# Attention: the maximum's pieces of two heads on separate halves of the array, diagonal blocks of four heads in one bank, pieces dealt out by columns

## The reference

```python
qkv = x @ w_qkv                                   # (4, 2048, 3, 16, 16)
Q, K = apply_rope(Q), apply_rope(K)
attn = jnp.einsum('bqhd,bkhd->bhqk', Q, K) * scale
attn = jnp.where(causal, attn, NEG_INF)
attn = jax.nn.softmax(attn, axis=-1)              # over 2048 keys, causal
out = jnp.einsum('bhqk,bkhd->bqhd', attn, V).reshape(B, S, dim)
return out @ w_proj + b_proj
```

## Time and profile before

| what | us |
|---|---|
| median of three runs | 3551.72 |
| the profiled execution | 3548.13 |
| its span in the profile | 3546.4 |
| TensorE busy | 3175.5 (90%) |
| VectorE busy | 2645.6 (75%) |
| ScalarE busy | 1569.4 (44%) |
| GpSimd busy | 763.4 (22%) |
| attention, from its first instruction to the last output's division | about 324 to 2151 |
| of it: the first group's maxima | 339 to 426 |

### The profile page before, as it was taken

The page is one execution under the profiler, slowest core; times in us unless marked ns, Lnnn a source line. Parts: engine busy times, 40 slices in busy tenths (PEclk is TensorE's granted clock), DMA queues, the critical chain, the costliest instruction groups (busy, mean ns, idle before and its releaser), DMA issues. The chain is left out here.

```text
span 3546.4 us, 64058 instructions
## 1 busy us (share of the span) xinstructions
PE 3175.5 (90%) x18948; PEld 1799.1 (51%) x18948; DVE 2645.6 (75%) x6114; ACT 1569.4 (44%) x2096; POOL 763.4 (22%) x619
## 2 busy tenths in 40 slices
PE   5885999999999999999999996764599999799998
PEld 3552233333333333333333334554588888678787
DVE  4885888888887888878788833887477777566666
ACT  1442166666666666666566672111244444211111
POOL 1775000000000000000000002777332323333332
PEclk8997599999999999999999997665799999899999
DMA  1776111111111111111111104553554545322222
GB/s 66 190 206 192 42 31 46 45 54 47 38 39 45 54 47 42 36 45 54 47 44 35 34 7 110 171 165 121 171 163 151 162 152 163 115 89 89 89 89 71
DMA packets 372705, 315.08 MB, mean 89 GB/s; under 512 B 99436, under 2 KB 359000, under 8 KB 372440
## 3 DMA queue, kind: packets, MB, share of 16 engines
q1 hardware_dynamic: 360152, 278.26, 26.6%
q0 software_dynamic: 12288, 33.57, 2.8%
HBM read 194.27 MB, written 116.92 MB: 88 GB/s over the span
## 5 line engine op out<-in xcount | busy, mean ns | idle before, releaser
L820 ACT ACTIVATE probs<-ps_s 128x1024 f32<-128x1024 f32 (+3 forms) x1280 | 1083.5, 894 | 728.6 <-PE ps_s L957 475.1
L947 PE MATMUL ps_m<-k_st,q_st 96*128 96x512 bf16 (+3 forms) x2560 | 838.0, 363 | 47.9 <-POOL k_st L801 30.9
L957 PE MATMUL ps_s<-q_st,k_st 98*128 98x512 bf16 (+3 forms) x2560 | 714.4, 352 | 27.0 <-issue 20.3
L973 PE MATMUL ps_o<-probs,vs 128*32 128x512 f32 (+3 forms) x5120 | 605.0, 545 | 0.0
L845 DVE CUSTOM_DVE_ANT_0 masked<-ps_m,mask_qk 128x512 bf16<-128x512 f32 (+3 forms) x1024 | 462.5, 489 | 163.1 <-PE ps_m L947 150.9
L947 PEld LDWEIGHTS ps_m<-k_st,q_st 96*128 96x128 bf16 x2560 | 215.3, 97 | 715.7 <-DVE piece_late L848 205.7
L848 DVE TENSOR_REDUCE piece_late<-ps_m 128x1 f32<-128x512 f32 x768 | 473.1, 681 | 30.5 <-PE ps_m L947 29.8
L848 DVE TENSOR_REDUCE piece_rest<-ps_m 128x1 f32<-128x512 f32 x768 | 475.0, 682 | 27.5 <-PE ps_m L947 18.7
L1218 POOL MEMSET zeros<- 128x1024 f32 x1 | 1.0, 956 | 1815.1 <-POOLq L670 1815.1
L957 PEld LDWEIGHTS ps_s<-q_st,k_st 98*128 98x128 bf16 x2560 | 242.2, 98 | 247.5 <-ACT probs L820 67.7
L962 PE MATMUL ps_s<-mask_kq,ident_b 128*128 128x128 bf16 x1024 | 204.4, 219 | 0.0
(11 more groups left out here) (226 smaller groups left out, 5423.2 us busy)
## 6 DMA issues: line engine op xcount, KB each, us to landing
qk_parts<-parts SPq DMA_DIRECT2D x128, 192.0 KB, 2.9
k_st<-qk_parts SPq DMA_DIRECT2D x384, 64.0 KB, 2.3
q_st<-qk_parts SPq DMA_DIRECT2D x384, 64.0 KB, 2.3
x_r<-expert_rows SPq DMA_DIRECT2D x39, 512.0 KB, 4.5
expert_made<-made SPq DMA_DIRECT2D x39, 512.0 KB, 3.0
x_in<-in_L_attn_x_dram SPq DMA_DIRECT2D x32, 512.0 KB, 4.6
v_ones<-v_out SPq DMA_DIRECT2D x64, 256.0 KB, 4.7
vs<-v_ones SPq DMA_DIRECT2D x64, 256.0 KB, 3.6
```

The source lines that it names most:

```text
L820: act.activation(probs[:, u % PSLOTS, 2 * pair:2 * pair + 2, j * P:ST], ps_s[:, pair, :, j * P:ST], ACT.Exp, scale=SCALE).then_inc(exp_don ...
L947: pe.matmul(ps_m[:, bank, 0:w], q_st[0:ROWS, slot, h, qi * P:(qi + 1) * P], k_st[0:ROWS, slot, h, kt * ST:kt * ST + w], start=True, stop=T ...
L957: last = pe.matmul(ps_s[:, pair, hh, j * P:ST], k_st[0:ROWS + MROWS, slot, h, kc * P:(kc + 1) * P], q_st[0:ROWS + MROWS, slot, h, qt * ST ...
L973: last = pe.matmul(ps_o[h * VW:(h + 1) * VW, j * P:ST], vs[:, slot, kc, h * VW:(h + 1) * VW], probs[:, u % PSLOTS, h, j * P:ST], start=(kc ...
```

## The change

It does four things.

1. The rows of the stacks are laid out anew. The three products that weigh most stand together. For an even head they are rows 0 to 47; for an odd head rows 64 to 111, its other three products are rows 16 to 63, rows 0 to 15 are zero, and the maximum's two rows are 112 and 113 (96 and 97 for an even head). Each load of 16 rows takes two heads instead of four, so a region has 24 loads instead of 12. Rows from 96 on are set to one and rows 0 to 15 of odd heads to zero at the start: for slot 0 by VectorE, for slot 1 by GpSimd. SyncE's first load waits for VectorE's three.
2. A piece of 512 or 384 columns is now one matmul over 48 rows, with the three main products alone: the maximum need not be exact. Two heads, an even and an odd one, form a unit of two pieces, in two banks, one on array rows 0 to 63 and one on 64 to 127. TensorE starts a unit when the bank of its second piece is free.
3. Pieces no longer hold the diagonal block. What is left of 256 columns stands with two heads in one bank, of 128 columns with four, with all products. The 16 diagonal blocks of 128 stand with four heads in one bank and their own column in `piece_late` or `piece_rest`; the mask is a bf16 matmul of 512 columns by the identity. So VectorE has 140 plain reduces instead of 160 pieces, and the masked form is gone.
4. The order on TensorE: both scores' pairs of a position now stand together, and units stand in two slots of a position, ahead of the scores and ahead of the values. They are dealt out by columns (`work`, `width`) instead of by count.

```diff
@@ -43,9 +44,12 @@
-ROWS = 96
-QPART = (0, 0, 0, 1, 1, 2)
-KPART = (0, 1, 2, 0, 1, 0)
+QPART = (0, 0, 1, 0, 1, 2)
+KPART = (0, 1, 0, 2, 1, 0)
+MAIN = 3
+HEAD_ROWS = ((0, 16, 32, 48, 64, 80), (64, 80, 96, 16, 32, 48))
+SHIFT_ROW = (96, 112)
+MAX_BASE = (0, 64)
...
-    PIECES = [(kt, qi, h) for kt in reversed(range(NQ)) for qi in reversed(range(TPS * kt, NT)) for h in range(HG)]
-    LATE_END = max(i for i, (kt, qi, h) in enumerate(PIECES) if qi >= LATE)
-    LATE_LAG = 8
+    Piece = namedtuple("Piece", "qi col k0 w h n")
+    TRI = {True: NQ, False: NQ - 1}
+    WIDE = {1: HG, 2: HG // 2, 3: 1, TPS: 1}
+
+    def units_of(kt, qi):
+
+        w = min(TPS, qi - TPS * kt) * P
+        if w == 0:
+            out = []
+        else:
+            n = WIDE[w // P]
+            parts = [Piece(qi, kt, kt * ST, w, h, n) for h in range(0, HG, n)]
+            out = [parts[0:2], parts[2:4]] if n == 1 else [[part] for part in parts]
+        if qi < TPS * (kt + 1):
+            out.append([Piece(qi, TRI[qi >= LATE], qi * P, P, 0, HG)])
+        return out
+
+    UNITS = [unit for kt in reversed(range(NQ)) for qi in reversed(range(TPS * kt, NT)) for unit in units_of(kt, qi)]
+    FIRST_OF = {units_of(kt, NT - 1)[0][0]: kt for kt in range(NQ)}
+    LATE_END = max(i for i, unit in enumerate(UNITS) if unit[0].qi >= LATE)
+    LAST_LATE = UNITS[LATE_END][-1]
+    LATE_LAG = 3
...
-    LOADS = 2 * len(QPART)
+    LOADS = 4 * len(QPART)
...
+    def work(unit):
+        return sum((what.w * what.n if isinstance(what, Piece) else P) + P for what in unit)
 
     def plan_of(first, maxima):
 
 
-        spread = with_late(PIECES) if maxima else []
-        out = []
+        spread = with_late() if maxima else []
+        out = [[] for _ in range(2 * NPOS)]
+        width = [ST - P * max(0, kc - TPS * qt) + P for qt, kc in POSITIONS]
+        at = [0]
         for u in range(NPOS):
-            a, b = (len(spread) * (u - 1) // (NPOS - 1), len(spread) * u // (NPOS - 1)) if u else (0, 0)
-            now = spread[a:b]
-            if u == 1:
-                now = ["turn rest"] + now
-            if u == 3 and not first:
-                now = now + [("turn o", -1, NQ - 1)]
-            if u - 2 in LAST_OF:
-                now = now + [("turn o", 0, LAST_OF.index(u - 2))]
-            out.append(now)
+            at += [at[-1] + width[(u + 1) % NPOS], at[-1] + width[(u + 1) % NPOS] + width[u]]
+        total, past = sum(work(unit) for unit in spread), 0
+        out[1].append(["turn rest"])
+        for unit in spread:
+            out[min(m for m in range(1, 2 * NPOS) if at[m] * total >= past * at[2 * NPOS - 1])].append(unit)
+            past += work(unit)
...
+        if not first:
+            out[7].append([("turn o", -1, NQ - 1)])
+        for k, u in enumerate(LAST_OF[:-1]):
+            out[2 * (u + 2) + 1].append([("turn o", 0, k)])
...
-        mask_qk = sb("mask_qk", [P, ST])
-        masked = sb("masked", [P, BANKS, ST], BF16)
+        mask_qk = sb("mask_qk", [P, HG, P], BF16)
         mask_kq = sb("mask_kq", [P, P], BF16)
-        q_st = sb("q_st", [P, 2, HG, S], BF16)
-        k_st = sb("k_st", [P, 2, HG, S], BF16)
+        q_st = sb("q_st", [P, 2, 2, HG // 2, S], BF16)
+        k_st = sb("k_st", [P, 2, 2, HG // 2, S], BF16)
...
-                    for i, part in enumerate(which):
-                        sp.dma_start(stack[i * HD:(i + 1) * HD, slot, :, cols],
-                                     qk_dram[ds(g, 1), side, part, :, cols].rearrange("o (h d) t -> d (o h) t", d=HD)) \
-                            .then_inc(qk_in[slot][r], 16)
+                    for odd in range(2):
+                        for row, part in zip(HEAD_ROWS[odd], which):
+                            src = qk_dram[ds(g, 1), side, part, :, cols].rearrange("o (a z d) t -> d z (o a) t", d=HD, z=2)
+                            sp.dma_start(stack[row:row + HD, slot, odd, :, cols], src[:, odd, :, :]) \
+                                .then_inc(qk_in[slot][r], 16)
...
+            sp.wait_ge(blank, 3)
             for slot in range(2):
+                if slot == 1:
+                    sp.wait_ge(pool_own, 3)
...
-            pool.memset(mask_qk[:, :], 0.0).then_inc(pool_own, 1)
+            pool.memset(k_st[96:P, 1, :, :, :].rearrange("p z a t -> p (z a t)"), 1.0).then_inc(pool_own, 1)
+            for n, stack in enumerate((k_st, q_st)):
+                pool.memset(stack[0:HD, 1, 1, :, :].rearrange("p a t -> p (a t)"), 0.0).then_inc(pool_own, 1)
+            pool.wait_ge(pool_own, 3)
+            pool.memset(mask_qk[:, :, :], 0.0).then_inc(pool_own, 1)
             pool.memset(mask_kq[:, :], 0.0).then_inc(pool_own, 1)
-            pool.memset(piece_rest[:, :, :].rearrange("p n k -> p (n k)"), LOWEST).then_inc(init, 1)
-            pool.wait_ge(pool_own, 2)
-
-            pool.affine_select(out=mask_qk[:, ST - P:ST], in_=mask_qk[:, ST - P:ST], compare_op=ALU.is_ge, fill=NEG,
-                               base=0, pattern=[[-1, P]], channel_multiplier=1).then_inc(init, 1)
+            pool.memset(piece_rest[:, :, :, :].rearrange("p h n k -> p (h n k)"), LOWEST).then_inc(init, 1)
+            pool.memset(piece_late[:, :, :, :].rearrange("p h n k -> p (h n k)"), LOWEST).then_inc(init, 1)
+            pool.wait_ge(pool_own, 5)
+
+            pool.affine_select(out=mask_qk[:, :, :], in_=mask_qk[:, :, :], compare_op=ALU.is_ge, fill=NEG, base=0,
+                               pattern=[[0, HG], [-1, P]], channel_multiplier=1).then_inc(init, 1)
             pool.affine_select(out=mask_kq[:, :], in_=mask_kq[:, :], compare_op=ALU.is_ge, fill=NEG, base=0,
                                pattern=[[1, P]], channel_multiplier=-1).then_inc(init, 1)
-            pool.wait_ge(init, 3)
-            pool.memset(k_st[ROWS:ROWS + MROWS, :, :, :].rearrange("p s h t -> p (s h t)"), 1.0).then_inc(init, 1)
...
+            k_rows = k_st[96:P, 0, :, :, :].rearrange("p z a t -> p (z a t)")
+            v.memset(k_rows, 1.0).then_inc(blank, 1)
+            for stack in (k_st, q_st):
+                v.memset(stack[0:HD, 0, 1, :, :].rearrange("p a t -> p (a t)"), 0.0).then_inc(blank, 1)
...
-                kt, qi, h = what
-                w = min(ST, (qi + 1) * P - kt * ST)
-                dst = piece_late[:, h * TPS + qi - LATE, kt:kt + 1] if qi >= LATE else \
-                    piece_rest[:, h * LATE + qi, kt:kt + 1]
+                qi, col, k0, w, h, n = what
+                dst = piece_late[:, h:h + n, qi - LATE, col] if qi >= LATE else piece_rest[:, h:h + n, qi, col]
                 v.wait_ge(m_done, count)
-                if kt == qi // TPS:
-                    stand_alone(v, held)
-                    v.tensor_tensor_reduce(masked[:, bank, 0:w], ps_m[:, bank, 0:w], mask_qk[:, ST - w:ST], 1.0, LOWEST,
-                                           ALU.add, ALU.max, dst).then_inc(m_taken, 1)
-                else:
-                    v.tensor_reduce(dst, ps_m[:, bank, 0:w], AX.X, ALU.max).then_inc(m_taken, 1)
+                v.tensor_reduce(dst, ps_m[:, bank, 0:n * w].rearrange("p (n w) -> p n w", n=n), AX.X, ALU.max) \
+                    .then_inc(m_taken, 1)
...
+            def piece(what, bank, slot, turn):
+                qi, col, k0, w, h, n = what
+                if what in FIRST_OF:
+                    pe.wait_ge(qk_in[slot][FIRST_OF[what]], turn * (16 * LOADS))
+                for i in range(n):
+                    z, a = (h + i) % 2, (h + i) // 2
+                    rows = slice(MAX_BASE[z], MAX_BASE[z] + MAIN * HD) if n == 1 else slice(0, SHIFT_ROW[z])
+                    last = pe.matmul(ps_m[:, bank, i * w:(i + 1) * w], q_st[rows, slot, z, a, qi * P:(qi + 1) * P],
+                                     k_st[rows, slot, z, a, k0:k0 + w], start=(i == 0),
+                                     stop=(i == n - 1 and k0 != qi * P), skip_group_check=True)
+                if k0 == qi * P:
+                    last = pe.matmul(ps_m[:, bank, :], ident_b[:, :], mask_qk[:, :, :].rearrange("p h t -> p (h t)"),
+                                     start=False, stop=True, skip_group_check=True)
+                last.then_inc(m_done, 1)
...
+                    rows = SHIFT_ROW[h % 2] + MROWS
                     last = pe.matmul(ps_s[:, pair, hh, j * P:ST],
-                                     k_st[0:ROWS + MROWS, slot, h, kc * P:(kc + 1) * P],
-                                     q_st[0:ROWS + MROWS, slot, h, qt * ST + j * P:(qt + 1) * ST],
+                                     k_st[0:rows, slot, h % 2, h // 2, kc * P:(kc + 1) * P],
+                                     q_st[0:rows, slot, h % 2, h // 2, qt * ST + j * P:(qt + 1) * ST],
...
-                def some(todo, third):
-                    for idx, what in todo[len(todo) * third // 3:len(todo) * (third + 1) // 3]:
-                        pe.wait_ge(m_taken, freed(base, idx, before))
-                        item(what, g, g + 1, idx % BANKS, 1 - par, it + (1 + par))
-
```

(16 more changed lines are left out.)

68 lines of the change are left out of this document (36 added, 32 removed).

## The result

The changed kernel takes 3577.4 us (median of 4 runs, 3572.6 to 3583.9); the kernel before took 3551.6 beside it. The ratio on record is 1.0081, with a 95% interval of 1.0069 to 1.0094, and the two medians alone give 1.0073: **slower by 0.7 to 0.8%**, some 26 us. The forecast was 3562 (+11), the range 3512 to 3600, and the chances 0.41 slower against 0.40 faster. The profiled execution has 3572.6 us and a span of 3570.8, against 3548.1 and 3546.4.

A forecast was written before the change was run, and what follows sets the result against it. TensorE, 99% busy at full clock, bounded the steady part; the start and first group's maxima were priced apart. +11 +3.6 +10 -13 (15 rounds of -0.9) = +11.6 us; 3551.7 + 11, rounded, gave 3562 us, range 3512 to 3600.

The forecast's parts named there:

- first piece: At the start: held loads delay TensorE's first piece from 339.05 to 350.3, +11 us (+2 to +13).
- region 2's hole: At the start: region 2 lands 11.2 us later, less region 3's work worth 7.5; +3.6 us (0 to 5).
- the first group's maxima: Before the first scores: a pair takes 1.38 us against VectorE's 1.20, clock at half; +10 us (0 to 13).
- stream without waits: Steady part, TensorE per group: pieces' matmuls save 7.6 us, shape changes cost 6.0 (0 to 7.2).
- waits: Steady part, TensorE per group: +0.4 us for VectorE's banks (-1 to +3), +0.3 for ScalarE (0 to 1).
- loop's return: The round holding it has a 4.1 us hole, then a slow clock; claimed untouched by the change, no term.
- SyncE's doubled loads: Issuing a region takes 11.2 us instead of 5.6; hidden in the steady part, the rest maxima's store some 11 later.
- Rival B: Steady part: the halves of a pair don't overlap, +11 us a group, 3727 us; chance 0.04.
- Rival A: Steady part: row tiles cost no change of shape, or half of one, 3523 us; chance 0.33.
- Rival C: Steady part: the two-bank rule decides, a group's waits grow by 3 us more, 3607 us; chance 0.12.
- 106 to 107 apart: Sign in the steady part: "turn late" cuts 106 to 107 us apart instead of 107.4.
- "350" and "450": Signs at the start: TensorE's first piece near 350 us, the first scores near 450 instead of 425.9.

The follow-up runs named there:

- Kernel 2: The changed kernel, with TensorE waiting before each piece for that piece's own bank instead of a pair for its second piece's bank; 3573.4 us.
- kernel 3: The changed kernel, with the first loads of even heads (regions 3 and 2) issued ahead of the wait for VectorE's memsets; 3565.0 us.
- kernel 7: The changed kernel, with VectorE reducing only half of each piece of 512 or 384 columns; 3542.2 us.
- Kernel 6: The changed kernel, with no two pairs in one slot and three empty slots taking the pair of the slot behind; 3540.5 us.
- kernels 5 and 11: 5: the changed kernel with 32 more semaphore increments on TensorE at the stage's start, 3564.4 us; 11: the kernel before with 128, 3568.9 us.

## Why the prediction came out as it did

The direction was held at near even odds, so that it came true is mostly luck, and the time lay in the range. The forecast (whose own terms add up to +11.6, not 11) is 13 to 15 us short. The fifteen rounds alone came out 21 us dearer than forecast, +7.8 for -13; the first group and the stages behind gave 8 of it back. By the prediction's steps:

| term, us | predicted | measured |
|---|---|---|
| first piece | +11 | +10.1 |
| region 2's hole, and the first group's maxima | +3.6 + 10 | +10.7 |
| stream without waits, 15 x | -1.6 | -1.8 |
| waits, 15 x | +0.7 | +1.8 |
| loop's return (with the other irregular rounds) | 0 | +6.3 |
| last group and behind | 0 | -4.2 |

**The start**: right in its sum, with parts that cancel. The memsets took 6.88 + 1.76 + 1.76 = 10.4 us and not 13: 0.84 ns an element, GpSimd's own value and not the masked form's. The Trainium skill, VectorE: DVE Perf Modes, "Zero memsets can be issued as uint32 (trn2)", gives a memset one cycle per element whatever the type. The trace agrees that the type doesn't count (2048 uint32 and 8192 bf16 cost the same per element), and shows the 4096 bf16 zeros of a stack row issued as 2048 words. The rest went into gaps of 0.4 to 0.5 between the memsets, and a later begin (325.16 where I had 323.8); the landing took 1.8 us instead of 2.3.

**The first group**: the pair's wait is right to 0.01 us (1.38 said, 1.39 seen), and the half clock nearly: the granted clock was 0.57 over the stretch, 0.50 before. Kernel 2 puts the wait at 8.2 of the 10, and kernel 3 puts the hole at some 5 instead of 3.6. The two are 13.4 of 10.7 measured, so some 3 came back; VectorE's smaller work may be the reason, and no run shows it by itself.

**SyncE's doubled loads**: hidden, as said. The store of the rest maxima starts 8.1 us behind the return's first scores before and 19.4 behind them now (1324.19 to 1343.60), 11 later, as forecast, and nobody waits for it:

```profile
1343.60 3.08 SPq L776 DMA_DIRECT2D q_st<-top  x4
```

**The halves**: 3 ns between the two of a pair, 0.32 to the next matmul. Rival B is out. Rival A as well: a shape change into or out of the row halves costs 0.093 to 0.103 in each direction (row to full 0.103, row to columns 0.100, columns to row 0.098), and there are 140 a group, as counted. By the rule of the Trainium skill, TensorEngine Tiling (Array Packing), "Key Properties", a change of tiling mode drains the array. The trace doesn't show a drain as such, but it agrees in the price: row halves cost as much to enter and leave as the column tiles of the earlier trace rows. The stream of 22.0 + 6.0 us was thus right to 0.2 us a round.

**The waits** are the step that was mis-sized: "**+0.4** (-1 to +3)" for VectorE and "**+0.3** (0 to 1)" for ScalarE. I summed the gaps between TensorE's starts over a regular round, less each matmul's own width and 0.093 to 0.103 for each change of shape (the table behind kernel 7): 3.3 us before, 5.1 after, so +1.8 for +0.7. ScalarE's part is +1.0 for +0.3. I had priced it on the mean, 1.94 of exponentials in 2.16; it came in three places, between the two pairs of scores at the first position of a query tile, behind the narrow diagonal positions: 0.47 each (the trace's own idle is 0.31). VectorE's part, with the small ones, is +0.8 for +0.4. Its places were named, and the worst of them was nearly right, 1.38 for 1.3 where two pairs stand in the slot of "turn rest". The split holds as far as the unit prices do, some 0.005 us a matmul. Rival C, "the waits of a group grow by 3 us more", was the forecast's +0.7 plus 3; measured was +0.7 plus 1.1. So the regular round came out at +0.1 and not -0.9: 15 us of the error. Kernel 6 shows that ScalarE's part was a matter of places alone.

**The loop's return** is the second failure: "nothing here touches it". The five returns took 7.2 us more: two holes with 4.8 us together where one of 4.1 stood, more time at half clock behind them, and a wait of 1.0 for a bank. The last belongs to the pairs; of the holes, kernels 5 and 11 show that a few instructions ahead of the loop move the returns in both directions. The earlier trace rows showed a hole put down to "issue", which nothing in the kernel's text explains; a stall without a releaser should have been a term with bounds, not a constant. The Trainium skill has the rule, and I hadn't weighed it: Runtime: NRT & Kernel Launch, "Instruction fetch mechanics", says that instructions come in blocks of 16 KiB, 256 instructions, and that a taken branch to a block no longer held must wait for its fetch. The traces agree. In all seventy returns of the fourteen traces one packet of 16 KB on an instruction queue (q8 in the DMA view, 7 or 8 such packets a round) ends 1.6 to 2.0 us before TensorE goes on. Before, it runs from 1301.79 to 1302.77, and TensorE, idle since 1300.33, goes on at 1304.45. In the changed kernel it runs from 1321.54 to 1322.42, TensorE is idle from 1321.92 and goes on at 1324.19; a second runs from 1324.65 to 1325.89, and the second hole ends at 1327.25. Every second hole of "issue" has such a packet of its own, 1.2 to 1.6 us ahead of its end. The length of the first hole goes with the packet's start: in holes of 3.5 to 4.5 us it starts 0.9 to 1.6 us after TensorE ran dry, in the short ones (1.7 to 2.3 us, and one of 2.9) 0.4 to 1.0 us before. What sets that start is open. That the second hole comes where the loop's top lies one matmul before the end of a block fits the single matmul between the holes; no run moved the top by a single instruction, so that detail stays argued.

Of the signs named ahead, "106 to 107 apart" missed by half a microsecond (107.47), and it was the sign with the most weight; "350" and "450" were met at 349.13 and 447.13.

## What to carry to other kernels

A faster form of an operation in a full stream is worth its own price less that of its mode changes, and then its places decide: the same pairs gave +0.1 us a round in one order and -1.8 in another. Price the waits for every engine that the new order meets, place by place and not on the mean: the waits for ScalarE, nearly all at three positions of forty, were worth as much here as a third less work on VectorE. And a loop's return belongs in the sum with bounds whenever the program's length changes; a few idle instructions ahead of the loop are a cheap thing to try.

## What the runs showed that I had not expected

- The hole at a loop's return took 1.85, 2.24, 2.28 + 2.49, 4.12 and 4.07 + 2.89 us in programs that differ only in length and order, and the half clock behind it lasted from nothing to 13.7 us.
- Thirty-two increments that compute nothing made one kernel 10 us faster in its rounds and left another as it was; 128 made it 21 us slower, and its first piece came 4.7 us later.
- A VectorE with a third less to do moved a 107.5 us round by only 1.7 us, though it was the engine that freed the banks. Other places for the same work gave 1.8, out of quite other waits: those for ScalarE.
